# Four matmul operands of a graph kernel move to another place modulo 128 bytes in SBUF

## What is computed

```python
x = _layernorm(x + _L0_gnn_ref(x, adj, L0_gnn_W), axis=-1)
x = _layernorm(x + _L1_gnn_ref(x, adj, L1_gnn_W1, ...), axis=-1)
x = _layernorm(x + _L2_gnn_ref(x, nodemask, adj, adj, L2_gnn_W_qkv, ...), axis=-1)
x = _layernorm(x + _L3_gnn_ref(x, adj, L3_gnn_W_qk, L3_gnn_W_v), axis=-1)
```

## The kernel before, in words

| tensor | start, modulo 128 bytes |
|---|---|
| `w0`, `w123`, `wqkv`, `wout`, `w3` | 32 |
| `adjT`, `fT`, `sup`, `hidT`, `x2T`, `v_sb`, `qkT` (queries and keys) | 96 |
| `oT`, `x3`, `x3T`, `k3`, `ident` | 64 |
| `work` (probabilities) | 0 |

## Time and profile before

### The profile page before, as it was taken

How to read it: one execution, slowest core, us unless ns; L and a number is a source line. 1 busy time by engine, 2 the same in 40 slices (tenths; PEclk the granted TensorE clock), 3 DMA queues, 4 the chain that set the end, 5 groups by cost and what they waited for, 6 DMA issues and landing times.

```text
span 1305.0 us, 30579 instructions
## 1 busy us (share of the span) xinstructions
PE 1286.8 (99%) x10987; PEld 1183.3 (91%) x10987; DVE 1201.8 (92%) x3821; ACT 911.5 (70%) x2445; POOL 139.8 (11%) x265
## 2 busy tenths in 40 slices
PE   8999999999999999999999999999999999999997
PEld 7899999999999999999999999999999999999985
DVE  6898999999999999999999999999999999998996
ACT  5767667677667677676677676776676776776773
POOL 0000110101110101101001101011101011110011
PEclk9999999999999999999999999999999999999999
DMA  5211011110111100111100111101111101110000
GB/s 192 68 34 35 1 43 43 42 42 2 43 42 43 42 26 18 43 42 43 42 16 28 43 42 43 42 2 42 43 42 43 34 11 42 43 42 10 10 10 25
DMA packets 51588, 49.03 MB, mean 38 GB/s; under 512 B 7920, under 2 KB 51184, under 8 KB 51440
## 3 DMA queue, kind: packets, MB, share of 16 engines
q1 hardware_dynamic: 51440, 47.08, 11.8%
HBM read 38.68 MB, written 8.39 MB: 36 GB/s over the span
## 4 chain that ended last, share of the span: by engine, by line
PE 96%; DVE 1%; DMA 1%; ACT 1%; issue 0%; POOL 0%; SPq 0%; POOLq 0%; DVEq 0%; ACTq 0%
PE psum L1473 63%; PE psum L1487 13%; PE psum L1717 9%; PE psum L1679 8%; PE psum L1768 1%; PE psum L1771 1%; DMA adj_sb<-in_adj 1%; PE psum L1780 1%; PE psum L1790 0%; POOL rstd L333 0%; ACT fT_h L373 0%; DVE bn L854 0%; SPq L233 0%; DVE x L888 0%; ACT adj_junk L429 0%
## 5 line engine op out<-in xcount | busy, mean ns | idle before, releaser
L521 ACT ACTIVATE work<-work,shift 128x256 f32<-128x256 f32 x512 | 253.8, 499 | 35.5 <-DVE shift L1017 35.5
L1036 DVE SCALAR_TENSOR_TENSOR work<-work,rsum,extra 128x256 f32<-128x256 f32 x512 | 216.5, 473 | 0.2
L373 ACT ACTIVATE work<-psum 128x512 f32<-128x512 f32 x256 | 138.3, 595 | 76.6 <-PE psum L1487 72.6
L1017 DVE CUSTOM_DVE_ANT_0 work<-psum,minus_big 128x256 f32<-128x256 f32 x512 | 189.3, 416 | 0.9 <-PE psum L1679 0.9
L373 ACT ACTIVATE sup_h<-psum 128x512 fp32r<-128x512 f32 x128 | 75.7, 591 | 156.6 <-PE psum L1473 156.6
L330 POOL TENSOR_TENSOR mv<-mv,eps 128x2 f32<-128x2 f32 x128 | 32.4, 253 | 1151.1 <-DVE mv L875 1151.1
L1473 PE MATMUL psum<-x2T_h,wqkv_h 128*128 128x256 f32 x512 | 145.0, 283 | 0.0
L1473 PE MATMUL psum<-x2T_h,wqkv_l 128*128 128x256 f32 x512 | 142.4, 278 | 0.0
L1473 PE MATMUL psum<-x2T_l,wqkv_h 128*128 128x256 f32 x512 | 142.4, 278 | 0.0
L1487 PE MATMUL psum<-ident,work 128*128 128x128 f32 x1024 | 129.5, 275 | 0.0
L1717 PE MATMUL psum<-work,v_sb 128*64 128x256 f32 x1024 | 124.7, 386 | 0.0
(11 more groups left out here) (134 smaller groups left out, 3753.6 us busy)
## 6 DMA issues: line engine op xcount, KB each, us to landing
xT_sb<-in_xT SPq DMA_DIRECT2D x32, 256.0 KB, 2.7
adjT_sb<-in_adjT SPq DMA_DIRECT2D x32, 256.0 KB, 3.2
adj_sb<-in_adj SPq DMA_DIRECT2D x32, 256.0 KB, 4.7
x_sb<-in_x SPq DMA_DIRECT2D x32, 256.0 KB, 4.8
out<-y_sb SPq DMA_DIRECT2D x32, 256.0 KB, 4.3
work<-in_L_gnn_W_qkv SPq DMA_DIRECT2D x1, 1536.0 KB, 9.2
mask_row<-in_nodemask SPq DMA_DIRECT2D x32, 32.0 KB, 4.5
w_raw<-in_L_gnn_W SPq DMA_DIRECT2D x3, 256.0 KB, 6.3
```

What stands on the lines that cost most here:

```text
L373: return nc.scalar.activation(dst, src, ACT.Copy, scale=scale)
L521: last = nc.scalar.activation(prob[:, p % 2, i, h], prob[:, p % 2, i, h], ACT.Exp, bias=shift[:, p % 2, h, i:i + 1], scale=-1.0, accum_out ...
L1017: last = V_.tensor_tensor_reduce(out=prob[:, p % 2, i, h], in0=bank(SCORES[p] + h)[:, i * N:(i + 1) * N], in1=minus_big[:, g % 2, i], scal ...
L1036: last = V_.scalar_tensor_tensor(out=prob[:, p % 2, i, h], in0=prob[:, p % 2, i, h], scalar=rsum[:, p % 2, h, i:i + 1], in1=extra[:, g % 2 ...
```

## The change

It adds three unused tensors as spacers and makes each row of `qkT` 64 bytes longer than what is used of it. It also states three pairs of waits in the other order.

```diff
+    HALF = 16
...
         fT = [sb(f"fT_{s}", [P, FT, N], F32R) for s in "hl"]
+
+        sb("space_0", [P, HALF])
         sup = [sb(f"sup_{s}", [P, NT, F], F32R) for s in "hl"]
+        sb("space_1", [P, HALF])
...
-        qkT = [sb(f"qkT_{s}", [P, 2, 2, N], F32R) for s in "hl"]
+        qkT = [sb(f"qkT_{s}", [P, 2, 2, N + HALF], F32R)[:, :, :, 0:N] for s in "hl"]
...
+        sb("space_2", [P, HALF // 2])
         oT = [sb(f"oT_{s}", [P, PAIRS, N], F32R) for s in "hl"]
...
                 pe.wait_ge(dve_xT, once(g))
+                reuse(pe, act_self, once(g - 1))
                 reuse(pe, dve_scores, nth2(g - 2, 0, 1))
-                reuse(pe, act_self, once(g - 1))
...
                 if p == 3:
+                    pe.wait_ge(dve_sup0, once(g + 2))
                     pe.wait_ge(act_sup0, once(g + 2))
-                    pe.wait_ge(dve_sup0, once(g + 2))
...
                     if p == 0 and h == 1:
+                        pe.wait_ge(dve_qk, nth(g, p + 2))
                         pe.wait_ge(act_qk, nth(g, p + 2))
-                        pe.wait_ge(dve_qk, nth(g, p + 2))
```

## The result

The changed kernel takes 1298.2 us, the median of 6 runs (1296.4 to 1301.6), against 1309.3 for 6 runs of the kernel before: a ratio of 0.992, 95% interval 0.9908 to 0.9932. The profiled execution took 1296.4 us with a span of 1294.6 at a granted clock of 0.999, against 1306.8 and 1305.0 before. That is 11.1 us gained by the medians, 10.4 by the profiled executions, where the prediction had 14.2.

The account below looks back on a forecast made before the run. PE, busy 99%, was taken as the bound. Terms of 459 ns a graph, x 32, made 14.7 us; less 0.5 for tight places, 14.2 gained from 1306.8 gave 1292.6, plus 2.3 for the median 1294.9 us; range 1285 to 1307.

Parts of the forecast that it names:

- The cause: Distance modulo 128 between moving and stationary places sets PE's pitch; rival that it does not: 1309 us, chance 0.11.
- project_out and gcn_out: 24 and 12 matmuls a graph, from 119.6 and 119.2 ns to 113.3: 151 and 71 ns gained.
- good level: The lower pitch of 256-column matmuls at distance 64, about 113.3 ns.
- aggregate: 12 matmuls a graph, from 120.0 ns to the good level: 80 ns gained, 30 at the middle level.
- middle level: The higher pitch at distance 64, about 117.5 ns; rival that changed blocks reach only this: 1304.4 us, chance 0.14.
- hidden(1): 12 matmuls behind support0 HI, which is on the middle level: 80 or 30 ns a graph, 55 taken.
- hidden(0): 12 matmuls behind qk(1), which is on the middle level: 66 or 16 ns a graph, 16 taken.
- scores: 24 pairs of row halves a graph at 117.5 ns a pair: 101 ns gained or 0, 50 taken.
- tail_project: 12 matmuls of 384 columns a graph: between 0 and 114 ns gained, 36 taken.
- Good blocks tip over: Rival: shifted PE phase drops self_product, support(1), support(2), qk(2), qk(3) to the middle level: 1312.5 us, chance 0.08.
- The waits: The three exchanged waits on PE cost nothing, all being fulfilled before PE came to them.
- the pieces: Two-piece copies into qkT: 36 ns a graph on DVE, beside PE; rival that DVE pays: 1301 us, chance 0.06.

Follow-up runs that it names:

- e1: Kernel of its own, writing zeros: PE alone runs matmuls at chosen operand distances modulo 128 bytes; 256 columns took 113.3 ns at 64, 120.0 at 0.
- e7: The changed kernel with the value columns of wqkv in a tensor of their own, so values runs at distance 0: 1305.18 us, ratio 0.9979 to the kernel before.
- e8: The changed kernel with wqkv moved from place 32 to 96 and x2T from 96 to 32: 1303.29 us, ratio 0.9966 to the kernel before.
- e10: The changed kernel without the gap in qkT, so scores is at distance 0 again: 1303.79 us, ratio 0.9968 to the kernel before.
- e9: Kernel of its own, writing zeros: 12 matmuls at distance 64, a disturbance, then 24 more; behind one matmul at distance 0 all 24 took 117.8 ns.
- e4: The kernel before with only the gap in qkT: 1307.28 us, ratio 0.9984.
- e11: The changed kernel with tail_project HI put behind support(0) HI: 1299.43 us, ratio 0.9937 to the kernel before.
- e5: The kernel before with only the three exchanged waits: 1306.77 us, ratio 0.9996.
- e6: The changed kernel with its three waits back in the old order: 1297.81 us, ratio 0.9925 to the kernel before.
- e2: The kernel before with only the two spacers around sup, old waits and no gap in qkT: 1306.9 us, ratio 0.9985.
- e3: The kernel before with only the spacer ahead of oT (space_2), which moves oT, x3T and k3: 1302.84 us, ratio 0.9958.
- e12: The changed kernel with tail_project LO ahead of support(0) LO and ACT's qkv copy ahead of its sup copy: 1299.68 us, ratio 0.9932.

## Why the prediction was right, and where it wasn't

The measured 1298.2 us lie within the range of 1285 to 1307, 3.3 us above the 1294.9 of the forecast.

**The cause** held. PE's pitch hangs on the distance of the two places modulo 128 bytes (e1). The rule that was weighed against it, "Loading the next tile's weights doesn't steal SBUF read bandwidth from the running matmul" (the Trainium skill, "TensorE: Matmul & The Clock Gate", Part 2), would have given 1309 us. The runs disagree with it for these float32r matmuls: 6.7 ns in 120 go with the place of the weights alone, in e1 with no other reader beside PE.

**project_out and gcn_out**, 151 and 71 forecast, 150 and 71 measured. They were read from the right rows, and the argument (neighbours on the good level) was the right kind. e7, e8 and e10 show how thin it was: each put project_out on 117.8 with its places untouched.

**aggregate** is the step that failed most: 80 forecast, 11 measured. That "the block behind them, qk(3), is entered without loss" said nothing of how aggregate itself is entered. It fell on the middle level, and its first gap grew from 130 to 140 ns. By e9 a matmul of 512 columns is enough to drop a level, and values LO, four of them, stands right ahead of it. But gcn_out stands behind values HI in the same manner and is at 113.3, so what e9 shows doesn't carry over as it is.

**hidden(1)**, 55 taken between 80 and 30: 26, the lower end. **hidden(0)**, 16 taken: 5. Both stand behind a block at 117.5 to 118, and both ran at 117.7 on: the half between the two levels was met by neither.

**scores**, 50 taken between 101 and 0: about 14, and 33 in e4. In scores(2) with scores(3) the pitch behind the first pair is 117.8 ns a pair in both traces, in scores(0) with scores(1) it went from 119.5 to 118.2. So scores stayed at the middle level, where it had been at distance 0 already. In e1 row halves at distance 64 took 117 to 123 ns for the first pairs and 113.3 from the sixth pair on, and about 118 and 117.5 at 32 and 96. Its series at distance 0 ran mostly at half the clock and gives no comparison.

**tail_project**, 36 taken: the low part gained 17, the high part lost 34, since qk(0) ahead of it gained 39 and x3T comes no sooner. ACT's copy and the weight load that needs it, in the kernel after:

```profile
614.53 0.59 ACT L378 ACTIVATE x3T_h<-psum 128x512 fp32r<-128x512 f32 x1
...
615.17 0.19 PEld L1478 LDWEIGHTS psum<-w_h,x3T_h 128*128 128x128 f32 x1
```

The copy ends at 615.12, and from the first start of tail_project HI to the second it is 0.24 us, where 0.18 is the rest of the block; e11, where the wait is gone, confirms it. The busy line doesn't show such a wait (PE 39.28 of 39.28), since the matmuls ahead are still in flight, so "no idle time" was no proof that nothing is waited for; e5 and e6 had to show it for the three waits. Where the gain of the low part comes from is not clear: e1 has 384 columns at 173.3 ns at distance 32 and 174.7 at 64. That PE's gain turns into a wait was the right kind of worry at the wrong place: the prediction looked at support0 LO, where nothing happened.

**Good blocks tip over** was a rival for a slower kernel. It happened in part: support(1) from the good level to 117.8, 42 ns. In e2 it happened to four blocks and took everything back. Its chance of 0.08 was too low for how close it lies, and its "against", that no entry becomes closer, argued from the wrong quantity. On the other side qk(0) tipped up, 39 ns, which no term had.

**The waits** and **the pieces** cost nothing, as said (e5, e6; 675 ns and 675). DVE followed, as said.

Together: 459 forecast, 299 measured. The shortfall is aggregate (69), tail_project (53), scores (36), hidden (40), support(1) (42), qk(2) (17) and qk(1) (10), less what untouched blocks gave (qk(0), values, support(0), self_product). The terms were taken as independent, and they are not: the slot's gains of e2, e3 and e4 are 0.02, 0.22 and 0.07 us, their sum 0.31, which is the whole change's 0.31 (as means of 27 slots 0.00, 0.20 and 0.05, together 0.25 of 0.30); but sup and oT together give 0.17, less than oT alone. The agreement of the sum is then a coincidence. That the time came out within the range owes most to project_out and gcn_out, 221 of the 299, and as e10 shows it was luck that project_out stayed on the good level.

**Left open.** Why a given boundary in this kernel raises or drops the level (gcn_out against aggregate, project_out in e7 and e8, qk(1) in e12): e9's list of widths names no pattern that covers them. Why values gained 37 ns with untouched places: it gained 33 in e2 and nothing in e3 and e4, so the gain came with the move of sup, which values doesn't read. What sets the level behind a pause. What in the chip makes 113.3 and 117.8 wasn't reached by any run.

## What to carry to other kernels

Where PE sets the end, divide the starts of matmuls by their number, block by block; if equal shapes show unequal pitches, look at the places of both operands modulo 128 bytes, and try 64 for 256 columns of float32r. For 512 columns 0 was the cheapest alone, but in the kernel the move cost 7 us through the blocks around it (e7). Then measure the whole change in one run and read the pitch of every block, touched or not, since the neighbours' levels move by as much as the term itself: a single part of such a change, tried alone (e2), can look worthless. Forecast such a gain at one level or the other, and not at a mean of the two.

## What the runs showed of the hardware that was not expected

- A level is kept as far as was tried: 36 matmuls in a row at 117.8 behind 12 at distance 0 (e1), and through every first exchange of roles (e1, e9). Entries at distance 64 from equal pauses ran at either level (e1, e9).
- Distance 88 reaches 113.3 too, after some 7 matmuls; 512 columns are cheapest at distance 0 (226.7 against 233.4).
- PE's clock halved while PE was busy. Windows of e1 over its series of 192 columns, then of 128 columns:

```profile
349.40:368.40 19.00, 16.28 (x132) 15.04 (x132) 0.00 (x0) 2.39 (x4) 0.00 (x0) 1.00 0.00 1
...
380.60:397.00 16.40, 15.24 (x66) 14.22 (x66) 0.00 (x0) 1.00 (x2) 0.00 (x0) 0.50 0.01 1
```

In the second PE is busy 15.24 of 16.40 us and the granted clock is 0.50, the level of 1.2 GHz, with 213 ns a matmul where 111.6 stood at the full clock. The four series of 192 columns and the first of 128 had run at the full clock, with the same pauses of about 0.7 us; the matmuls went from 111 to 213 ns within the second series of 128. The clock came back in the first series of row halves, where the distance of two pairs went from 213 to 119 ns. The kernel itself didn't show it (0.999).
